# One row load issued ahead of the routing tables, and five normed tiles turned through DRAM and VectorE

## The reference

```
x = x + L0_xattn(layernorm(x), ctx, ctx)        # softmaxes over heads and tokens, no weights
x = x + L0_ffn(layernorm(x), U1, V1, U2, V2)    # low rank, silu gate
x = x + L1_xattn(layernorm(x), ctx, Wq, Wk, Wv, Wo)  # 16 heads of 96, 4 shared keys/values
x = x + L1_ffn(layernorm(x), gate_w, bias, Wg, Wu, Wd, Sg, Su, Sd)
# L1_ffn: scores = sigmoid(x @ gate_w.T) + bias; the best 4 of 16 experts per token, weights
# normed to 1; out = sum over them of w * (silu(x Wg) * (x Wu)) Wd, and a shared expert (Sg, Su, Sd)
```

## Time and profile before

| | us |
|---|---|
| median of 3 runs (lowest, highest) | 708.01 (707.88, 709.03) |
| the profiled execution, its own time | 709.7 |
| its span on the core | 707.6 |
| PE / DVE / ACT / POOL busy in the span | 679.5 / 346.2 / 193.3 / 176.3 |
| mean granted TensorE clock | 0.987 |

### The profile page before, as it was taken

How to read it: one execution, slowest core, us unless ns; L and a number is a source line. 1 busy time by engine, 2 the same in 40 slices (tenths; PEclk the granted TensorE clock), 3 DMA queues, 4 the chain that set the end, 5 groups by cost and what they waited for, 6 DMA issues and landing times.

```text
span 707.6 us, 9751 instructions
## 1 busy us (share of the span) xinstructions
PE 679.5 (96%) x2460; PEld 404.0 (57%) x2461; DVE 346.2 (49%) x838; ACT 193.3 (27%) x543; POOL 176.3 (25%) x226
## 2 busy tenths in 40 slices
PE   9999899999999999999999999996999999999992
PEld 7555343446777777777776785673444444444440
DVE  3998433544234446576665767454233333333331
ACT  4453322212244433323333242220111111111110
POOL 2354210101000000013513314255033332332342
PEclk9999999999999999999999999999899999999996
DMA  9999997133300110001104105312866757768544
GB/s 335 406 421 420 422 421 325 45 125 114 134 0 1 33 58 0 1 16 46 60 2 149 59 2 175 123 75 63 280 172 114 179 103 181 183 130 235 91 74 59
DMA packets 60403, 103.19 MB, mean 146 GB/s; under 512 B 7200, under 2 KB 32544, under 8 KB 59712
## 3 DMA queue, kind: packets, MB, share of 16 engines
q1 hardware_dynamic: 30608, 73.61, 27.8%
q0 software_dynamic: 8816, 18.00, 12.8%
q10 hardware_dynamic: 20944, 11.15, 5.4%
HBM read 46.60 MB, written 56.26 MB: 145 GB/s over the span
## 4 chain that ended last, share of the span: by engine, by line
PE 79%; issue 8%; DVE 4%; DMA 3%; SPq 2%; ACT 1%; POOL 1%; POOLq 0%; DVEq 0%; ACTq 0%
PE ps L1196 48%; PE ps L1377 9%; PE ps L1346 4%; PE ps L1184 4%; PE ps L1362 4%; PE ps L1295 3%; PE ps L1296 3%; PE ps L1305 3%; DVE rq L964 2%; DMA r<-in_ctx 2%; DMA out<-rq,sidx 1%; PE ps L1315 1%; SPq L412 1%; SPq L418 1%; PE ps L1237 1%
## 5 line engine op out<-in xcount | busy, mean ns | idle before, releaser
L1196 PE MATMUL ps<-kv,rq 128*128 x432 | 195.3, 601 | 6.0 <-SPq L520 5.4
L1196 PEld LDWEIGHTS ps<-kv,rq 128*128 128x128 f32 x432 | 79.8, 193 | 94.9 <-issue 94.7
L1196 PE MATMUL ps<-zT,r 128*128 128x256 f32 (+1 forms) x552 | 132.5, 395 | 0.9 <-ACT kv L697 0.9
L1196 PEld LDWEIGHTS ps<-zT,r 128*128 128x128 f32 x552 | 103.4, 190 | 24.5 <-issue 11.2
L1377 PE MATMUL ps<-r 128*128 128x512 f32 x192 | 85.1, 593 | 0.0
L624 POOL DMA_INDIRECT out<-rq,sidx x36 | 56.7, 1574 | 111.9 <-DMA out<-rq,sidx 83.3
L551 POOL TENSOR_SCALAR ve<-mv 128x1 f32<-128x1 f32 x32 | 7.2, 224 | 289.5 <-DVE mv L933 289.5
L735 ACT ACTIVATE r<-ps,snm 128x128 f32<-128x128 f32 x128 | 45.3, 366 | 82.4 <-DVE snm L1029 78.9
L1123 DVE TENSOR_TENSOR rq<-ps,rq 128x256 f32<-128x256 f32 x36 | 15.3, 424 | 104.3 <-ACT rq L787 104.3
L1377 PEld LDWEIGHTS ps<-r 128*128 128x128 f32 x192 | 35.2, 190 | 38.3 <-issue 38.3
L787 ACT ACTIVATE rq<-ps 128x256 f32<-128x256 f32 x36 | 13.8, 384 | 125.0 <-PE ps L1196 115.1
(11 more groups left out here) (176 smaller groups left out, 844.9 us busy)
## 6 DMA issues: line engine op xcount, KB each, us to landing
slot_rows<-rq SPq DMA_DIRECT2D x4, 8192.0 KB, 50.7
kv<-in_experts SPq DMA_DIRECT2D x54, 256.0 KB
rq<-slot_rows ACTq DMA_DIRECT2D x136, 64.0 KB
r<-in_Wq SPq DMA_DIRECT2D x1, 3072.0 KB, 21.2
r<-in_Wo SPq DMA_DIRECT2D x2, 1536.0 KB, 6.4
r<-in_ctx SPq DMA_DIRECT2D x8, 256.0 KB, 8.3
xr<-in_x SPq DMA_DIRECT2D x8, 256.0 KB, 8.4
second_norm_rows<-zrow SPq DMA_DIRECT2D x8, 256.0 KB, 2.2
```

What stands on the lines that cost most here:

```text
L1196: mm = pe.matmul(out, lhs(k), rhs(k), start=(k == 0), stop=(k == n - 1))
```

## The change

Two parts.

The first routed tile's rows. `load_first_block` loads block 0 of `slot_rows` with addresses fixed in the program. SP issues it as soon as all rows are placed, ahead of its waits for the two tables; block 1 is read from `tab` and loaded as before.

The third norm of tiles 0 to 4 (`TURNED` = 5). VectorE writes the normed tile twice: to `zrow`, for GpSimd's scatter, and to `zquad` with its columns permuted so that the exchanged blocks come out in plain order. SP stores `zquad` and loads it back as in the second norm, and VectorE transposes it to `zT`. The four TensorE transposes and the ScalarE copy of these tiles go. `ln_t` of tiles 0 to 4 moves from n = 4j + 11 to 4j + 12, behind the division of that step; the gate's product waits for VectorE's transpose instead of ScalarE's copy. Tiles 5 to 7 stay as they were.

```diff
-        tail_of = ((10, 1, "ln_z"), (11, 2, "ln_t"), (12, 1, "gate"), (13, 1, "place"))
+        tail_of = ((10, 1, "ln_z"), (12, 0, "ln_t"), (12, 1, "gate"), (13, 1, "place"))
+        def by_dram(step):
+            return step[0] == "ln_t" and (step[1] == 2 or step[1] == 3 and step[2] < TURNED)
+        def load_first_block(eng):
+            for b in range(4):
+                eng.dma_start(xrow[b * QD:(b + 1) * QD, 0, :].rearrange("p (a e) -> p a e", a=4),
+                              quads_d[0, b, :, :, :]).then_inc(s_gx[0], 16)
...
             def turn_rows(j):
-                sp.wait_ge(s_z, LNN[("ln_z", 2, j)] + 1)
-                sp.dma_start(zrow_d[j % 2], zrow[:, LNN[("ln_z", 2, j)] % 2, :]).then_inc(s_zst[j % 2], 16)
+                z = LNN[("ln_z", 2 + j // J, j % J)]
+                sp.wait_ge(s_z, z + 1)
+                if j >= J:
+                    sp.wait_ge(s_zp, j - J + 1)
+                sp.dma_start(zrow_d[j % 2], zrow[:, z % 2, :] if j < J else zquad[:, :]).then_inc(s_zst[j % 2], 16)
...
             load_wo(1)
+            for j in range(4):
+                turn_rows(J + j)
             sp.wait_ge(s_q, 4 * G)
             sp.dma_start(wsh, ws_d).then_inc(s_ws, 16)
+            turn_rows(J + 4)
...
                 load_expert(sp, front_of[i], i * EW, s_wdma[i])
+            for k in range(TOPK):
+                sp.wait_ge(s_zs[k], 16 * J)
+            load_first_block(sp)
             sp.wait_ge(s_tabl, 1)
             loads = sp.value_load(head[0:1, 2:3], min_val=TOPK, max_val=E)
-
             sp.wait_ge(s_tab, 1)
-            for k in range(TOPK):
-                sp.wait_ge(s_zs[k], 16 * J)
-            for i in range(2):
-                block_of = sp.value_load(tab[0:1, i:i + 1], min_val=0, max_val=P)
-                load_block(sp, block_of, i, s_gx[i])
+            load_block(sp, sp.value_load(tab[0:1, 1:2], min_val=0, max_val=P), 1, s_gx[1])
...
+                    if layer == 3 and j < TURNED:
+                        dve.wait_ge(s_zt2, J + j)
+                        dve.tensor_scalar(zquad[:, :].rearrange("p (b k i) -> p k b i", b=4, k=KC),
+                                          xr[:, j, :].rearrange("p (k b i) -> p k b i", b=4, k=KC),
+                                          mv[:, col, 0:1], rstd[:, col:col + 1],
+                                          ALU.subtract, ALU.mult).then_inc(s_zp, 1)
-                elif kind == "ln_t" and step[1] == 2:
+                elif by_dram(step):
                     j = step[2]
-                    dve.wait_ge(s_zld, 64 * (j + 1))
-                    dve.wait_ge(s_pt, j // 4 + 1)
+                    dve.wait_ge(s_zld, 64 * (J * (step[1] - 2) + j + 1))
+                    if step[1] == 2:
+                        dve.wait_ge(s_pt, j // 4 + 1)
+                    else:
+                        dve.wait_ge(s_q, 4 * (j // 2) + 4)
+                        dve.wait_ge(s_pr, len(KVN))
```

More of the change, by code:

```diff
@@ L31 @@
 EARLY = 4
+TURNED = 5
 WARM = 12
@@ L205, in build @@
         s_z = sem("z_done")
+        s_zp = sem("z_permuted")
         s_zst = [sem(f"second_norm_stored{i}") for i in range(2)]
@@ L393, in build @@
                  ("sh_d", 4), ("sh_d", 5), ("sh_d", 6), ("sh_d", 7)]
+        def by_dram(step):
+            return step[0] == "ln_t" and (step[1] == 2 or step[1] == 3 and step[2] < TURNED)
         def order(kinds):
-            return {step: i for i, step in enumerate(p for p in prog if p[0] in kinds and p[:2] != ("ln_t", 2))}
+            return {step: i for i, step in enumerate(p for p in prog if p[0] in kinds and not by_dram(p))}
         TRN = order(("a_t", "ln_t", "t", "gate", "front", "place", "count"))
@@ L683, in _ @@
                     copied(step, ekT[:, j % 2, :])
-                elif kind == "ln_t" and step[1] != 2:
+                elif kind == "ln_t" and not by_dram(step):
                     copied(step, zT[:, :, step[2] * P:(step[2] + 1) * P])
@@ L984, in _ @@
                             dve.wait_ge(s_zst[old[2] % 2], 16 * (old[2] // 2 + 1))
-                        else:
+                        elif not by_dram(("ln_t", *old[1:])):
                             dve.wait_ge(s_tr, TRN[("ln_t", *old[1:])] + 1)
@@ L1187, in normed @@
             def normed(layer, j):
-                if layer == 2:
-                    pe.wait_ge(s_zt2, j + 1)
+                if by_dram(("ln_t", layer, j)):
+                    pe.wait_ge(s_zt2, J * (layer - 2) + j + 1)
                 else:
```

## The result

The changed kernel took 712.33 us (median of 12 runs, 707.36 to 716.67), the kernel before 708.89 us beside it (12 runs, 707.79 to 711.28): the ratio is 1.0043, with a 95% interval of 1.0026 to 1.0059. It is slower by 3.4 us, where 703.3 us and "faster" were forecast. The profiled execution took 712.36 us with a span of 710.3, against 709.7 and 707.6.

The account below looks back on a forecast made before the run. TensorE, busy 96% of the span, was taken as the bound; -2.2 + 1.1 - 1.5 - 3.0 = -5.6 us gave 704.1 from the profiled 709.7, 702.4 from the median 708.0. Forecast between them: 703.3 us, range 700.3 to 707.3.

Parts of the forecast that it names:

- Tiles 0, 2 and 3 have the same pattern: Gates in the attention: as at tile 1 (step 16), VectorE's transpose ends 1.5 us before the gate, so no wait.
- The five transposes: Second attention: removing five tiles' transposes at 0.43 us each from a full TensorE counts whole, -2.2 us.
- Tile 4's gate: Step 28 in the attention: the transpose ends after the gate is due, so TensorE waits, +1.1 us (0.7 to 1.6).
- Tile 3: Its gate in the attention was to have slack like tile 1's, so TensorE would not wait there: 0 us.
- The trip: Turned tile's store and loads through DRAM: 5.4 us, up to some 8 beside scatters, hidden within 9.4 us, costing nothing.
- the prediction's second estimate: Trip through DRAM under scatters: HBM access at high load makes two transfers in a row 3.6 us longer.
- turned tiles late: Rival in the attention, 8%: the trip beside GpSimd's scatters takes 13 us and TensorE waits at five tiles, 712.9 us.
- The shared weights: SP's queue: the shared expert's weights, issued at 381.3 behind tile 3's loads, land at 387.7 before use: 0 us, upper +2.
- fits by 3 us: SP's queue: the shared weights' load of 6.4 us lands at 387.7, its first product comes at 391.14 or 390.7.
- The stop: Way into the experts: the early block 0 load lets the first routed product start at 494.5, -1.5 us (0 to -5.4).
- The clock: Behind the stop at the experts: with the product back after 3.9 us the clock would not yet have fallen, -3.0 us.
- the first case: The forecast itself, all terms at attention and experts holding: 703.3 us, chance 42%, its own range 701.5 to 705.

Follow-up runs that it names:

- the experiment meant for it: The kernel before with GpSimd's last two tiles of id scatters held back until all but two of VectorE's last additions are done: 712.74 us, ratio 1.0167.
- part 1 alone: Against the kernel before, only tiles 0 to 4 turned through DRAM and VectorE, row loads as before: 705.82 us, ratio 1.0050.
- the kernel with the two extra moves: The mended kernel with expert weights counted before SP reads the tables and the first rows' turn ahead of VectorE's last two additions: 700.57 us, ratio 0.9983.
- part 2 alone: Against the kernel before, only block 0 of the rows loaded ahead of the tables: 702.73 us, ratio 1.0007; in a later group 708.37 us, ratio 0.9966.
- the mended kernel: The changed kernel with VectorE's transpose of a turned tile ahead of the query copies: 700.97 us, ratio 0.9979; in a later group 707.32 us, ratio 0.9961.

## Why the prediction was wrong

**The step that failed: "Tiles 0, 2 and 3 have the same pattern", with 1.5 us of slack in step 16.** That slack was counted from the division to the gate, as if the transpose stood directly behind the division. In steps 12, 16 and 20 the three query copies stand between; the order that I read, and printed, was that of step 28, which has none. The rows were there in the trace of the kernel before, in step 12 (tile 0) and in the same stretch as the earlier trace rows (tile 1):

```profile
294.43 1.31 DVE L1018 COPY rq<-ps 32x256 f32<-32x256 f32 x3 [1.15 <-PE ps L1196]
...
295.53 0.96 PE L1196 MATMUL ps<-gw,zT 128*128 128x16 f32 x8
...
327.20 1.31 DVE L1018 COPY rq<-ps 32x256 f32<-32x256 f32 x3 [2.49 <-PE ps L1196]
```

Step 16 again, in the kernel before of the group with the short stop:

```profile
326.46 1.31 DVE L1018 COPY rq<-ps 32x256 f32<-32x256 f32 x3 [1.15 <-PE ps L1196]
...
327.56 0.96 PE L1196 MATMUL ps<-gw,zT 128*128 128x16 f32 x8
```

Tile 0 by the trace that the prediction had: 294.43 + 1.31 + 0.71 = 296.45, 0.9 us behind the gate at 295.53; tile 2 gives the same (357.08 + 2.02 against 358.18). The measured 0.84 could have been worked out blind. Tile 1 by the same trace is 327.20 + 1.31 + 0.71 = 329.22, 2.3 us behind 326.96, where 1.67 was measured; by the short-stop trace it is 328.48, 0.9 us behind 327.56. Three gates, 4.15 us of shift in the changed kernel, were priced at nothing. The attention was forecast at -1.1 and came at +4.87 us: 4.15 of the difference is this, 1.7 the half clock behind tile 1's wait.

**And it hung the gate on a late release.** In step 16 of the kernel before the copies start 1.54 us after TensorE's next products (325.66), with the short stop 0.20 us after them (326.26), in the two traces of the changed kernel 1.02 and 2.51 us after them. Each time GpSimd's scatters of ids run in the same step. In step 12, where none run, it is 0.20 us in every trace. Of the 19 traces six are late in step 16, by 1.0 to 2.6 us: all those of the two groups with a median of 709 to 710 us, the same six that have the long stop. In the other 13 it is 0.20 us, beside the same scatters. The lateness cost the kernel before nothing, because nothing that TensorE needed soon stood behind the copies. The edit with the transpose ahead is immune: in the group with the long stop its copies wait 2.90 us for the same release, and its gate starts on time:

```profile
326.02 0.96 PE L1223 MATMUL ps<-gw,zT 128*128 128x16 f32 x8
327.29 1.31 DVE L1045 COPY rq<-ps 32x256 f32<-32x256 f32 x3 [2.90 <-remote]
```

This is the effect that I had read at the stop (TensorE's semaphores late beside the scatters) and not looked for in the attention. What makes it come in some groups is not shown, and the scatters alone don't bring it; the experiment meant for it missed.

**The other steps.**
- The five transposes: -2.2 forecast, 0.43 each measured (236.07 with four of them and no wait).
- Tile 4's gate: +1.1 forecast, 0.93 us idle and a shift of 1.20. Right, and its reason too. With the copies out of the way the attention came out at -0.98 and -0.95 us against the -1.1 forecast.
- Tile 3: no wait, right. Its transpose came at 392.26, just after its rows had landed (392.08), and the gate at 394.56.
- The trip: 5.4 us in the earlier trace rows, up to 8 taken as the bound. It is 6.7 us for tile 0, beside which no scatter ran, and 9.1 for tiles 2, 3 and 4 (second write done at 382.97, rows at 392.08 for tile 3), near the 9.0 of the prediction's second estimate (5.4 + 3.6); what makes it is not shown. The scatters alone don't explain it: tile 2's loads took 6.0 us from 354.12, and the last scatter beside them ended at 354.45. All of it is still inside the slack, so the rival "turned tiles late", which forecast 712.9 us, hit the number by the wrong mechanism.
- The shared weights: issued at 387.68, that is 382.0 without the 5.6 us by which the norm itself had shifted, against 381.3 worked out, and no wait in this trace. But the load was mis-sized: it landed 8.2 us after its issue and not 6.4 (7.7 to 9.7 in the traces that show it), and the "fits by 3 us" is not so. With the gate waits gone it landed at 388.83 and the product came at 388.97. TensorE waited 0.20 us there in part 1 alone, and in the kernel with the two extra moves:

```profile
389.56 1.78 PE L1223 MATMUL ps<-zT,r 128*128 128x256 f32 x7 [0.45 <-DMA r<-in_shared]
```

- The stop: -1.5 forecast; -1.93, -1.5 and -1.8 measured where the stop exists, nothing to win where it doesn't.
- The clock: -3.0 forecast, -1.56 in the profile after; beside the long stop of the later group +0.7 in part 2 alone and -0.7 in the mended kernel (10.18 and 8.82 us for the 16 records, 9.50 before). That it would not yet have fallen after 3.9 us was read from one row. In the other traces with the long stop the half clock began 2.1, 2.9, 3.6, 3.8 and 5.1 us after TensorE's last shared product, and it fell in or behind all four stops of 3.5 to 4.3 us. By the Trainium skill ("TensorE: Matmul & The Clock Gate", What's actually happening) the count runs freely; these rows agree with it. The prediction called the 3.0 "a chance and not a term" beside that rule, and its sum took it as a term all the same. And a new price came in: each gate's wait can bring the half clock too, 1.7 us in the profile after, three times in the second.
- The range: 700.3 us is given as the first case's lower end, which is 701.5 by the prediction's own words.

The sum as it came, for the profiled execution: -2.2 + 5.35 + 1.7 in the attention, -1.93 and -1.56 at the experts, and +1.10 ahead of the changed part, +2.5 in all where -5.6 was forecast.

## What to carry to other kernels

When an edit puts an instruction into an in-order engine, print the order at every step that takes it, not at one, and count from the instruction that will stand directly ahead of it, with its own releaser. A write that a busy engine waits for must not stand behind one that waits for that same engine. A stop read from one execution may belong to that group of runs until a second one shows it: here the kernel before had it in both profiles from groups of runs with a median of 709 to 710 us, and not in the profile from one of the four with 702 to 703 us. The version to keep is the change with the transpose ahead of the query copies, 0.2 to 0.4% faster than before on either kind.

## What the hardware showed that I had not expected

- TensorE's release reached VectorE 0.20 us after its next product in 13 traces and 1.0 to 2.6 us after it in the six of two other groups, in the same step, beside GpSimd's indirect scatters.
- SP's eight row loads in the kernel before took 4.43 us in the group with the short stop and 6.89 and 6.93 us in the two with the long one.
- Waits of TensorE of 0.84 us were followed by a half clock of 3.4 us at tile 1 in part 1 alone, and by none at tiles 0 and 2 of the same execution.
- A store of 256 KB and its four loads took 5.4 us in the second norm, 6.7 for tile 0 and 9.1 for tiles 2 to 4 of the third.
